# A four-layer transformer stack on one core: the shared expert's products with weights held still, and another order of work at the attention's opening

## What is computed

```python
x = x + jnp.tanh(g_xattn[0]) * _L0_xattn_ref(_layernorm(x), fside, ctx)      # quantised expert
x = x + jnp.tanh(g_ffn[0]) * _L0_ffn_ref(_layernorm(x), gate_w, ..., Ws3)    # 8 experts, top 2, and a shared one
x = x + jnp.tanh(g_xattn[1]) * _L1_xattn_ref(_layernorm(x), ctx, pos, pos, Wq, Wkv, Wout, bout)   # 32 heads, rotary
x = x + jnp.tanh(g_ffn[1]) * _L1_ffn_ref(_layernorm(x), router_w, w1, w2, w3)
# second layer:
h = silu(einsum('td,eid->tei', xt, W1)) * einsum('td,eid->tei', xt, W3)
y = einsum('tei,edi,te->td', h, W2, dw)                # routed experts
z = silu(xt @ Ws1.T) * (xt @ Ws3.T) @ Ws2.T            # shared expert
```

## Time and profile before

| | us |
|---|---|
| median of 3 runs | 1315.97 (1313.9 to 1318.4) |
| profiled execution, its own time | 1319.94 |
| its span | 1318.2 |
| PE busy in the span | 1159.4 (88%) |
| second layer's front, first product of a tile to last product | 241.8 to 324.5 |
| attention's opening to the first maxima | 561.9 to 622.5 |
| first maxima to first scores | 622.5 to 669.2 |

### The profile page before, as it was taken

The page is one execution under the profiler, slowest core; times in us unless marked ns, Lnnn a source line. Parts: engine busy times, 40 slices in busy tenths (PEclk is TensorE's granted clock), DMA queues, the critical chain, the costliest instruction groups (busy, mean ns, idle before and its releaser), DMA issues.

```text
span 1318.2 us, 16527 instructions
## 1 busy us (share of the span) xinstructions
PE 1159.4 (88%) x5247; PEld 509.5 (39%) x5309; DVE 831.5 (63%) x1289; ACT 666.5 (51%) x1175; POOL 397.7 (30%) x469
## 2 busy tenths in 40 slices
PE   5777776899999999958799989999999999889997
PEld 3454443555444444423232223222322222224543
DVE  6798765235555554136978888777877777714543
ACT  2565554565222222236456666666656666763452
POOL 4466531002322222043234432222222223102332
PEclk8988898999999999988899999999999999999999
DMA  7424125644544444194324342222222225400101
GB/s 239 134 99 136 56 89 183 234 178 163 208 135 142 155 149 132 62 292 101 107 80 138 114 122 79 83 81 80 75 86 79 80 81 65 51 5 9 38 35 48
DMA packets 111029, 145.79 MB, mean 111 GB/s; under 512 B 24952, under 2 KB 79736, under 8 KB 110440
## 3 DMA queue, kind: packets, MB, share of 16 engines
q1 hardware_dynamic: 91816, 113.47, 26.7%
q0 software_dynamic: 18368, 28.85, 8.5%
q10 hardware_dynamic: 768, 2.49, 0.6%
HBM read 99.54 MB, written 48.37 MB: 112 GB/s over the span
## 4 chain that ended last, share of the span: by engine, by line
PE 32%; DVE 9%; issue 8%; ACT 7%; POOL 1%; DMA 1%; ACTq 0%; POOLq 0%; DVEq 0%
PE PS L2888 7%; PE PS L2854 5%; PE PS L2789 4%; PE PS L2873 4%; PE PS L2813 3%; DVE a_top L3223 3%; ACT shared_w L3010 2%; PE PS L2391 2%; PE PS L2414 1%; ACT a_E L3010 1%; DMA a_attnT<-f_y,l_pos 1%; POOL a_K L2151 1%; PE PS L2018 1%; DVE a_early L3096 1%; PE PS L1984 1%
## 5 line engine op out<-in xcount | busy, mean ns | idle before, releaser
L3223 DVE TENSOR_REDUCE a_top<-PS 128x2 f32<-128x1024 f32 x256 | 309.2, 1223 | 84.9 <-PE PS L2873 78.5
L3010 ACT ACTIVATE shared_w<-PS 128x512 f32<-128x512 f32 x256 | 138.9, 596 | 74.7 <-PE PS L2854 73.8
L2854 PE MATMUL PS<-a_Q,a_K 99*128 99x512 bf16 (+1 forms) x468 | 156.9, 387 | 15.7 <-ACT a_E L3010 3.4
L3010 ACT ACTIVATE a_E<-PS 128x512 f32<-128x512 f32 x256 | 138.8, 596 | 61.1 <-PE PS L2854 57.9
L1502 PE MATMUL PS<-f_W,f_GT 128*128 x312 | 141.3, 596 | 0.0
L2873 PE MATMUL PS<-a_K,a_Q 64*128 64x512 bf16 x512 | 100.8, 390 | 13.4 <-DVE a_top L3223 7.0
L1931 POOL TENSOR_TENSOR a_qf<-a_qf,a_tab 128x512 f32<-128x512 f32 x15 | 19.1, 1272 | 279.9 <-DVE a_swapped L3125 279.9
L2854 PEld LDWEIGHTS PS<-a_Q,a_K 99*128 99x128 bf16 (+1 forms) x512 | 44.1, 97 | 151.2 <-issue 49.6
L1558 DVE TENSOR_TENSOR f_H<-f_SG,PS 128x256 f32<-128x256 f32 x39 | 16.4, 421 | 115.3 <-ACT f_SG L1542 115.3
L1502 PEld LDWEIGHTS PS<-f_W,f_GT 128*128 128x128 f32 x312 | 56.7, 191 | 57.2 <-issue 57.2
L2789 PE MATMUL PS<-a_xT,a_early 128*128 128x512 f32 x128 | 72.4, 662 | 2.2 <-ACT a_qf L2982 0.8
(11 more groups left out here) (381 smaller groups left out, 2085.7 us busy)
## 6 DMA issues: line engine op xcount, KB each, us to landing
f0r_raw<-in_L_ffn_W_dram SPq DMA_DIRECT2D x24, 512.0 KB, 4.0
a_K<-k_parts SPq DMA_DIRECT2D x192, 64.0 KB, 2.3
a_Q<-a_q_parts SPq DMA_DIRECT2D x186, 64.0 KB
f_y<-f_Y SPq DMA_DIRECT2D x39, 256.0 KB, 2.0
v_units<-V SPq DMA_DIRECT2D x16, 512.0 KB, 2.9
a_V<-v_units SPq DMA_DIRECT2D x16, 512.0 KB, 3.5
k_parts<-f_k_parts SPq DMA_DIRECT2D x16, 384.0 KB, 3.4
a_q_parts<-a_parts SPq DMA_DIRECT2D x16, 384.0 KB, 2.8
```

What stands on the lines that cost most here:

```text
L2854: nc.tensor.matmul(PS[:, 4 + h % 2, :], K6[k][0:rows_, o, head // 2, kt * P:(kt + 1) * P], Q6[k][0:rows_, o, head // 2, :], start=True, st ...
L3010: nc.scalar.activation(E[step % 2][:, h, :], PS[:, 4 + h % 2, :], ACT.Exp).then_inc(exp_done, 1)
L3223: nc.vector.tensor_reduce(top[:, h - h % 2:h - h % 2 + 2, t], PS[:, 2 * pair:2 * pair + 2, :], AX.X, ALU.max).then_inc(maxed, 1)
```

## The change

In the front, the shared expert is no longer computed tile by tile. `hidden(j, b, i)` computes one half (128 columns) of the hidden layer for a whole batch, with the weights as stationary operand and the batch's 512 rows moving; the result comes out already turned, so that the turn and its copy go. The downs of four tiles then follow in `rows`, beside the fills. The order of fills, turns, router steps and downs changes with it.

In the opening: the gather ring has four slots; SP loads the late rows in four parts, holds Wq back until x tile 0 is added and everything else until tile 2 is added; batch 0's statistics are taken tile by tile as its rows come; its turned parts alternate between two banks; statistics and normalisation of batch 1 go to later slots (statistics to slots 8 to 13 of turn (-1, 3), normalisation into turn (0, 0)); late steps and fills are laid out anew.

```diff
-            tile(0, lambda: logit(1), None)
-            tile(1, None, None)
+            hidden(0, 0, 0, lambda: logit(1), nothing)
+            hidden(1, 0, 1, nothing, nothing)
             turn(2)
-            tile(2, lambda: logit(2), None)
+            rows(2, (0, 1), lambda: logit(2), nothing)
             turn(3)
-            tile(3, last_logits, None)
-            tile(4, None, count)
-            tile(5, None, None)
-            tile(6, None, place)
-            tile(7, None, None)
+            rows(3, (2, 3), last_logits, nothing)
+            hidden(4, 1, 0, nothing, count)
+            hidden(5, 1, 1, nothing, nothing)
+            rows(6, (4,), nothing, place)
+            rows(7, (5, 6), nothing, nothing)
+            down(7)
...
+            def up(b, i):
+                n = b * IC + i
+                if n:
+                    pe.wait_ge(silu_ready, n)
+                for m, done in enumerate((gate_done, up_done)):
+                    for c in range(DC):
+                        last = nc.tensor.matmul(PS[:, 5 + m, :], shared13[:, c, m * I + i * P:m * I + (i + 1) * P], of_batch(b)[:, c, :],
+                                                start=(c == 0), stop=(c == DC - 1))
+                    last.then_inc(done, 1)
...
-        rows = Combine(nc, sb, sem, X, F32, weights, pos, ffn_gate, ys, 3, [attnT[1][:, d, :] for d in range(DC)])
+        rows = Combine(nc, sb, sem, X, F32, weights, pos, ffn_gate, ys, 4, [attnT[1][:, d, :] for d in range(DC)])
...
-                (-1, 2): {4: downs(2) + ups(3), 5: [("g", 3, 0), ("y", 2, 0)] + ups(4), 6: [("t", 3, 0), ("g", 4, 0)] + downs(3),
...
+                (-1, 2): {4: ups(2, [2, 3]) + ups(3), 5: [("g", 2, 0), ("t", 2, 0)] + downs(2), 7: [("y", 2, 0), ("g", 3, 0)],
...
             late.load(sp, 0)
+            sp.wait_ge(rows.tile_added, 1)
             sp.dma_start(wq, Wq.rearrange("(c p) n -> p c n", p=P)).then_inc(wq_loaded, 16)
...
+                    else:
+                        sp.wait_ge(rows.tile_added, TB - 1)
+                        sp.dma_start(tbias[:], bout.partition_broadcast(P)).then_inc(tbias_loaded, 16)
...
-            rows.vector(v, 2)
-            rows.vector(v, 3)
+            first_tile(3)
+            first_norm.wait()
```

More of the change, by code:

```diff
@@ L837, in fills_in_front, with front, hidden, rows @@
             return FILLS * (0, 1, 3, 4)[n]
-        def front(first_set, turn, logit, tile, choose, count, place):
+        def front(first_set, turn, logit, up, down, set_of, choose, count, place):
+            def hidden(j, b, i, beside, behind):
+                up(b, i)
+                beside()
+                for f in fills(j)[:DC]:
+                    set_of(f)
+                behind()
+                for f in fills(j)[DC:]:
+                    set_of(f)
+            def rows(j, tiles, beside, behind):
+                for n, t in enumerate(tiles):
+                    down(t)
+                    if n == 0:
+                        beside()
+                    for f in fills(j)[n * FILLS // len(tiles):(n + 1) * FILLS // len(tiles)]:
+                        set_of(f)
+                behind()
+            def nothing():
+                pass
+            def last_logits():
+                logit(3)
+                choose()
             turn(0)
@@ L1092, in _ @@
-            front(first_set, turn, logit, tile, lambda: None, lambda: router.tensor(pe), lambda: router.tensor_place(pe))
-            down(NS - 1)
+            front(first_set, turn, logit, up, down, lambda f: turned.tensor(pe, f),
+                  lambda: None, lambda: router.tensor(pe), lambda: router.tensor_place(pe))
 class Router:
@@ L2946, in _ @@
             late.take(act, 1)
-            late.silu(act, 2)
             def turn(b, c):
```

229 lines of the change are left out of this document (113 added, 116 removed).

## The result

The changed kernel takes 1310.0 us (median of 7 executions, 1303.4 to 1314.5) beside 1316.7 for the kernel before on the same chip: ratio 0.9947, 95% interval 0.9929 to 0.9964. It is 6.7 us faster; the forecast was 1296.4, with a range from 1288 to 1307. The direction holds, the size is a third of what I gave (19.6 us from the old median, 20.3 from this one). The profiled execution of after took 1311.2 us, its span is 1309.5, against 1318.2.

What follows compares the result with a forecast made beforehand. PE, busy 88% of the span, was taken as the bound, with idle time and half clock in the opening. 1319.94 - 3.6 (front) - 13.6 (to first maxima) - 2.4 (to scores) = 1300.3; median-adjusted by 4.0: 1296.4, range 1288 to 1307.

Steps and rivals of the forecast that it cites:

- the hole's 2.91 us: Front, tile 1: PE's wait for the third weight set would close, winning 4.5 us with the half clock after it.
- the 4.45 us: Front: the next set's fills can start about 4.45 us after the fourth fill, from one issue plus one landing.
- the two waits: Front: new PE waits for weight loads, 1.85 us ahead of set 7 and 0.9 ahead of set 8, together 2.75.
- 9 us before 586.1: Opening: tile 3's gathered rows would land at 577 instead of 586.1, between bounds of 575.6 and 580.7.
- 2.6 won: Opening: batch 0's four parts, turned through two banks, would take 4.6 us instead of 7.2.
- the choice of 4.7 us of waits: First maxima to first scores: waits chosen as 4.7 us beside 39.6 of work, stretch 44.3, 2.4 us won.
- Scores begin 16.0 us sooner: Attention: the first scores would start 16.0 us earlier, from the opening's 13.6 and the next stretch's 2.4.
- I count them at nothing: Turns after the first scores: batch 1's normalisation replaces two tiles' added rows at no cost; about 2.3 us if that fails.
- E: Rival: no change to tell, the opening's gain eaten in turn (0,0) by maxima's store and load; 1314 us, chance 0.04.
- C: Rival: the late chain bounds the stretch after the first maxima, waits stay 13 us; 1304.7 us, chance 0.14.
- B: Rival: opening gathers stay slow, tile 3 lands at 580.7, 4 to 6 us less won; 1301.5 us, chance 0.17.
- D: Rival: query stores wait because SP sits in the keys' loads, first maxima near 625; 1321 us, chance 0.03.

Runs made afterwards that it cites:

- e15: The kernel before the change, unchanged, profiled a second time: 1318.2 us (one execution).
- e2: The old front with the new opening and new attention turns: 1311.0 us, ratio 0.9936 to the kernel before.
- e14: The changed kernel, unchanged, profiled and timed again: 1310.2 us, ratio 0.9949 to the kernel before.
- e1: The new front with the old opening and old attention turns: 1315.0 us, ratio 0.9983 to the kernel before.
- e11: The changed kernel with POOL's last product of the front on 1 of its 512 columns, the rest uncomputed: 1309.4 us, ratio 0.9951.
- e12: The changed kernel with tile 6's products ahead of the last set's first half and tile 7's ahead of its second: 1310.1 us, ratio 0.9933.
- e7: The changed kernel with e6's edit, the second query load behind tile 2's take, and batch 1 normalised at positions 8 to 11 of (0,0): 1305.1 us.
- e8: The changed kernel without SP's two waits for added rows, so its loads aren't held back: 1309.9 us, ratio 0.9939.
- e9: The changed kernel with batch 1 normalised at positions 0 to 3 of turn (0,0) instead of 4 to 7: 1306.9 us, ratio 0.9933.
- e6: The changed kernel with batch 1's statistics at position 6 of turn (-1,2) instead of 8 to 13 of (-1,3): 1305.6 us, ratio 0.9902.
- e3: The changed kernel with batch 1's statistics, normalisation and bias back in turn (-1,3), its turns and row adds as before: 1309.9 us, ratio 0.9944.
- e10: The changed kernel with e6, e9, the query load behind tile 2's take, and tile 3's downs and tile 4's ups before the first maxima: 1301.4 us.
- e13: The changed kernel with e10 and e12 together, gate 6 at position 6 instead of 7, turn 7 at 14 instead of 13: 1298.1 us, ratio 0.9853.

## Why the prediction was wrong

Two steps failed. One is a cover: what follows the first scores was counted at nothing, and cost 2.9 us up to the second store, 1.6 of it by batch 1's normalisation and 1.3 by half clock. The other is the distance between two sets' loads in the front, taken as 4.45 us where it is 5.0 to 5.3. The opening's term was mis-sized besides. The terms are set against means from the table. Old front: before, e15, e2; new front: after, e14, e1. Old opening and what follows: before, e15, e1; new: after, e14, e2.

```
term                              forecast   measured   missing
front                               -3.6       -1.7       1.9
start of opening to first maxima   -13.6      -10.4       3.2
first maxima to first scores        -2.4       -1.1       1.3
first scores to second store         0         +2.9       2.9
behind the second store              0         +1.7       1.7
sum                                -19.6       -8.6      11.0
```

The experts' stretch is left out: it has 237.4 us with the old front and 237.9 with the new, all of it from e14's 239.0. The medians differ by 6.7 and not 8.6 us, which is within the spread of these parts from one execution to the next. None of the three signs that the prediction named for being wrong came: the gathers took under 9 us, the queries' store did not wait for SP, and PE's waits for late gates sum to 4.4 us. They watched the steps that held.

**Front: the distance between loads was taken too short.** The turns of H went as forecast, and of the hole's 2.91 us 0.55 stay. The step that failed is the 4.45 us from a set's fourth fill to the first fill of the next. In after it is 5.3 us ahead of set 7 and 5.0 ahead of set 8, and the same in e11. Two things were missing from it: the set's first transfer takes 0.41 us to issue (306.26 to 306.67), and the second lands 4.7 us after its issue begins (306.67 to 311.36), where 0.47 + 4.0 were counted; the 4.0 of the earlier trace rows is the landing of a set's third transfer, the only one whose landing the trace of before has. By these distances the two waits are 2.7 and 1.4 us instead of 1.85 and 0.9. The measured 2.64 only looks like the forecast 2.75, since another wait, for POOL's product (1.25 us, counted at nothing), lies in the same hole: together they are 3.9 us, and with POOL's product out of the way the load waits alone are 3.75 (e11). So POOL's product cost the front nothing that the load would not have cost. From set 7 on the front goes at the pace of the weights' loads: work behind the last load costs in full (e12, 2 us) and work ahead of it next to nothing (e11). My own arithmetic of distances between sets said this, and I used it only for the two waits.

**Opening: the chain right, a reason wrong, the term mis-sized.** "9 us before 586.1" was 8.1; "2.6 won" by two banks was 3.3 (3.9 us from 583.39 to 587.30 against 7.2). Two things were missing from the term. The execution of before had its rows at 29.1, two others at 27.4 and 25.6: I subtracted from a slow draw. And the forecast left the queries 10.5 us from their store to the first maxima (598.4 to 608.9), while their store, load and landing alone take 11.2 (595.72 to 606.96 in e7): the count of half a us for what ACT and down(2) win had no room. The reason given for the early rows, SP's holding back, was not it (e8): it brought tile 0's rows forward by 2.6 us, and tile 3's by 0.4 to 1.2. That tile 3's rows came near the forecast (578.0 for 577) is thus in part luck. The last gather was issued at 571.28 as forecast (571.4), and landed 6.8 to 7.7 us later in the three profiles, where 5.6 were counted.

**Second stretch: the choice of 4.7 us of waits.** Its work I had at 39.6, and the busy time is 40.1 (at a granted clock of 0.95, so a little of it is half clock); the rest is 5.4, so the choice of 4.7 was near. The mistake is in the end of the term: it stops at the first scores, which the change had moved against the other work. "Scores begin 16.0 us sooner" was to be the gain for good; they began 12.9 us sooner, and at the second store 10.0 were left (681.23 for 691.27).

**"I count them at nothing": the step that failed, and the largest single one.** Batch 1's normalisation and bias are 5.0 us of DVE in (0,0) in place of 3.0 of rows. The bias stands behind the second store, as the rows did; the four normalised parts (0.55 us each), put at positions 4 to 7, stand ahead of it, while DVE was idle 4.47 us at positions 0 to 2. The text even named the price if the cover fails, 2.3 us; it was 2.9. The traces show where it lies. The store goes out right behind POOL's rotation of the next queries (L1927 to L1940), which starts when DVE has shuffled them (L3165); the turned maxima had been copied 0.8 us before. The shuffle starts 15.8 us after the first scores in after (656.30 to 672.13), and 13.3 in before (669.23 to 682.56). Of these 2.5 us, about 1.2 are two of the normalised parts with their reciprocal, which stand ahead of the shuffle, and 1.3 are the half clock of the queries at 657.44 (3.29 for 1.98). The last 0.4 lie on POOL: two instructions of the rotation take 1.45 and 1.51 us beside the other two parts, but 1.28 and 1.27 in before, and 1.27 both in e9.

e9 shows the place: with the parts at positions 0 to 3 these 0.4 and PE's waits are gone, and 1.3 of the 2.9 us come back. e6 shows that the statistics of the same batch were in the wrong place too (ahead of gate 6), e3 that undoing the move altogether gains nothing. The half clock of the queries is gone in e7, e10 and e13. e7, which has the parts behind the shuffle and the queries at full clock, takes 22.1 us for this stretch, as before the change: with both causes away nothing of the 2.9 is left. What brings the clock down was not isolated: e6 and e7 have the same waits ahead of the queries (1.43 or 1.44 and 0.55 us), and the queries take 3.45 us in the one and 1.98 in the other.

**Behind it.** The tail is 174.6 to 175.7 us in nine runs, 176.0 and 176.7 in two, 177.0 to 177.2 in four, 179.1 in two; the same instructions. The 60 us from the last store on, in e6 (tail 175.5) and in after (177.1), by windows:

```profile
1125.93:1185.93 60.00, 52.57 (x242) 19.59 (x245) 23.77 (x66) 32.67 (x60) 6.35 (x11) 1.00 0.13 19
```

```profile
1132.42:1192.42 60.00, 53.36 (x239) 19.58 (x238) 23.32 (x65) 32.69 (x60) 6.33 (x11) 0.94 0.13 19
```

The clock differs, 1.00 against 0.94, and so does the time of the tail. All five profiles of the changed opening as it is have 177.0 to 179.1 (after, e14, e2, e11, e12), of the old one two have 174.9 and one 176.7; whether that is more than chance stays open, since e9 and e8, which differ by little, have 174.6.

**The rivals.** E (1314) came nearest to the 1310.0 in time, C (1304.7) next. C (waits as before, ACT's fills) did not come: what is not busy in that stretch is 5.4 us, not 13, and 4.4 of it are PE's waits for late gates. E had the place, turn (0,0), with the wrong thing in it: VectorE's own work, not the store of the maxima. B (tile 3's rows at 580.7) and D did not come.

## What to carry to other kernels

A gain of an early start lasts only if the work that was moved out of the way finds idle time elsewhere: give each moved piece a place in the timeline, not only a turn, and look at what stands behind it on its engine (here the shuffle, the cut and the gates). Measure a stretch between marks that the change doesn't move against each other, and take the base from more than one execution where a stretch hangs on transfers. In a chain that goes at the pace of loads, move work from behind the last load to the waits ahead of it; to shorten work ahead of it does nothing. And take the distance between loads from the trace, from the end of the work that frees the buffer to the start of the work that needs the next load: a sum of one issue and one landing left out 0.8 us of 5.3.

## What the hardware showed

- **GpSimd beside VectorE.** POOL's product takes 1.27 us alone and 3.12 when it begins inside a 2.28 us instruction of DVE; on one column it still takes 2.05, from 301.92 to 303.97, and DVE's instruction ends at 303.93 (e11). In the full case POOL's product ends 1.13 us after DVE's instruction (308.30 after 307.17), and DVE's next one took 1.87 us instead of 0.80. So it is not a slower pace for both, one waits for the other. By the Trainium skill, page "SBUF — State Buffer", section "Who interferes with whom", the two share a pair of ports that an instruction holds for its whole length; the rows agree.
- **Half clock after short waits.** PE came back at half clock after waits of 2.47 us (606.11, 3.78 us for 1.98) and 2.24 us (e11, 4.38 for 2.81), and at full clock after 2.25 us (647.57, 0.44 us for two turns). The granted clock was 0.50 from 606 to 608 and 1.00 from 648 to 650. The waits of 2.47 and 2.24 us so cost 1.7 times their length, that of 2.25 its length. Over the executions of after, 1303.4 us went with a mean granted clock of 0.973 and 1314.5 with 0.963.
- **Issuing is work.** Six loads cost ACT 2.7 to 2.8 us in which it computes nothing (602.80 to 605.58 in after); behind them the take of tile 2 came 2.5 us late.
